# One ring of seven PSUM banks for scores, maxima and all stages, and an exponential for each head

## The chip, the core and the metric

The kernel runs on one core of one Trainium2 chip. TensorE multiplies matrices into PSUM (8 banks, each 128 partitions by 512 fp32), ScalarE computes the exponentials and other activations, VectorE reductions and element-wise work, GpSimd small steps of the layer norms and gates, SyncE issues the DMAs. The engines run their own queues in order and meet at semaphores. The metric is the device time of one execution in microseconds, as the median of several runs.

## The reference

Four layers in a row on x (4 batches, 1024 tokens, 256 features), all in fp32: a diffusion-transformer block with self-attention (16 heads of 16, a mask, rotary positions), cross-attention to 77 context tokens and an MLP; a mixture of three experts with a gate; a second such block without mask; and a last cross-attention. What matters here is the self-attention of the first and third layer:

```python
def _L2_xcond_ref(x, c, context, ...):
    x_norm = modulate(_ln(x), shift_a, scale_a)
    qkv = x_norm @ W_qkv + b_qkv
    q, k, v = jnp.split(qkv, 3, axis=-1)           # each to B, 16 heads, N, 16
    attn_w = jax.nn.softmax(jnp.einsum('bhqd,bhkd->bhqk', q, k) * scale, axis=-1)
    attn_out = jnp.einsum('bhqk,bhkd->bhqd', attn_w, v)
    x = x + gate_a[:, None] * (attn_out.transpose(0, 2, 1, 3).reshape(B, N, H) @ W_proj + b_proj)
    ...                                            # cross-attention, then the MLP
```

The mask of the first layer leaves few live keys; the program looks at it at run time and takes, with these inputs, a branch that works on the last 256 keys alone.

## The kernel before

**Stages.** The program is a preparation (to about 110 us of the trace), the first layer with few keys (region `l0_`, to about 1118), the experts (`M`, to about 1712), and the third and fourth layer (region `l2_`, to the end). In a region every engine walks the same list of tokens, `R.order`, and does its own part of each. The list is made beforehand by a planner (`overlapped`), with a cost for each token, so that the slots of self-attention alternate with the other stages: projections (`qk`, `v`, `oP`), transposes (`lnT`, `oT`), cross-attention (`cq`, `cm`, `cn`, `cs`, `cp`, `ct`) and MLP (`m1`, `m2`). The order comes from costs and dependencies only, and the list is the same before and after the change.

**A slot.** Four heads of a group are done side by side, head j on rows 32j to 32j+31 of the array. A slot with number t handles one tile of 128 keys against 512 queries. TensorE runs in it, in `slot` of `region_pe`: the scores of heads 0 and 1 (`scores(t, 0)`); for a group further on, another score product of heads 2 and 3 whose row maximum is wanted (`fill`, keys "max"); the product of the slot before with V (`pv(t - 1)`, into the accumulator, bank 7); the scores of heads 2 and 3; the maxima's products of heads 0 and 1. ScalarE makes the exponentials of the scores into `PB` (named big in the trace), VectorE reduces each "max" tile to its row maximum (`max_halves`, or `row_max` with few keys). After the last tile of a group ScalarE copies bank 7 out (`o_T`), a "tail" entry transposes it, and "nm" entries transpose the maxima.

**Banks.** Banks 0 and 1 hold the scores of two heads at a time: TensorE writes both, signals `s_full` (scores_T_full), one ACTIVATE of 128 x 1024 reads both and signals `ex` (exp_done), and only then may TensorE write the next pair (`pe.wait_ge(R.ex, R.pairs[t, half] - 1)`). Banks 2 to 6 are a ring for everything else. Each use of a bank is an entry with a running number n (`R.number`), in the order of the list; it takes bank n mod 5 of the ring, and TensorE waits in `take` until the entry 5 before has been read. Readers signal `ring_free`, TensorE `ring_full`.

**Direct slots.** Where a slot with scores is followed directly by another with no other token between them, it is in `R.single`: its heads 2 and 3 then go to two ring entries and have an exponential of 512 columns each (line 1847), and only heads 0 and 1 use banks 0 and 1 and the pair exponential (line 1842).

**Lines.** Every matmul of the helper `mm` has line 884; 1842 and 1847 are the exponentials of self-attention, 1889 those of cross-attention, 1821 the copies, 1901 the MLP's gelu; 1524 and 1522 the maxima, 1666 the cross maxima, 1589 the rows of a layer norm. ScalarE holds one table of functions at a time; going from gelu to exponential puts an ACT_TABLE_LOAD ahead of the ACTIVATE.

## Time and profile before

| | |
|---|---|
| Median of 3 runs | 3743.86 us (3739.93 to 3747.18) |
| Profiled execution | 3739.93 us, span 3738.1 us |
| TensorE busy | 3403.1 us, 91% |
| VectorE busy | 1830.6 us, 49% |
| ScalarE busy | 1394.8 us, 37% |
| Mean granted TensorE clock | 0.927 |

The profiled execution is one of the three runs. A busy share says how long at least one instruction of the engine was in flight; matmuls overlap, so TensorE's is an upper bound of its work. PE is TensorE's matmul, PEld its weight load, which can run while a matmul does. In the rows, the figure in brackets behind an instruction is the idle time of its engine just before it, and the name behind the arrow is what ended it; "issue" means that the profile shows nothing that was waited for. In fp32 each matmul of the program shows as two.

### The profile page before, as it was taken

The numbers are of one execution on the slowest core, as the hardware profiler recorded it, in microseconds if no ns is written. First come the engines' busy times: TensorE is split into PE (matmuls) and PEld (weight loads), VectorE is DVE, ScalarE is ACT, GpSimd is POOL, SyncE is SP. The second block draws the span as 40 slices with busy tenths as digits, with TensorE's granted clock in tenths as the row PEclk, the third lists the DMA queues.
The fourth block names the chain that finished last, engine by engine and source line by source line (L and its number), as shares of the span: only waits on it lengthen the run. The fifth ranks groups of instructions, "written<-read, shape, count | busy, mean of one in ns | idle before, by whom it ended". The sixth has DMA issues, their size and how long they took to land.

```text
span 3738.1 us, 49981 instructions
## 1 busy us (share of the span) xinstructions
PE 3403.1 (91%) x20564; PEld 1880.3 (50%) x20564; DVE 1830.6 (49%) x3806; ACT 1394.8 (37%) x2043; POOL 242.8 (6%) x214
## 2 busy tenths in 40 slices
PE   5798989989889999998999899999999999998887
PEld 2554665646475666665433344434354343543464
DVE  3775554452312233226766655566555665553323
ACT  0243435444312222211455444443544445445332
POOL 0100100010100000001000100000100001000010
PEclk7898989989789999998899998999999999999797
DMA  5100000002000000001000000000000000000000
GB/s 180 60 1 5 8 19 4 19 5 89 15 21 0 1 1 1 0 1 52 1 1 1 7 1 3 15 15 7 1 3 15 15 7 1 4 15 15 1 1 12
DMA packets 57258, 58.06 MB, mean 16 GB/s; under 512 B 17728, under 2 KB 51248, under 8 KB 56764
## 3 DMA queue, kind: packets, MB, share of 16 engines
q1 hardware_dynamic: 57028, 54.79, 4.8%
q8 instruction: 169, 2.77, 0.3%
q14 instruction: 61, 0.50, 0.0%
HBM read 46.89 MB, written 7.89 MB: 15 GB/s over the span
## 4 chain that ended last, share of the span: by engine, by line
PE 80%; ACT 9%; DVE 8%; issue 2%; DMA 1%; SPq 0%; POOL 0%; DVEq 0%; ACTq 0%
PE ps L884 74%; ACT big L1842 6%; PE ps L1058 2%; DVE row_max_cross L1666 2%; ACT probs L1889 2%; PE ps L1180 1%; PE ps L1038 1%; DVE max_halves L1524 1%; PE ps L1049 1%; DVE big L1672 1%; ACT L1842 1%; DVE bn_stats L1576 0%; DVE xn_tok L1589 0%; DMA big<-in_L_xcond_bss_kv 0%; DVE bn_stats L1555 0%
## 5 line engine op out<-in xcount | busy, mean ns | idle before, releaser
L884 PE MATMUL ps<-big 32*128 32x512 f32 (+2 forms) x5760 | 920.2, 622 | 59.5 <-ACT big L1842 32.4
L1842 ACT ACTIVATE big<-ps 128x1024 f32<-128x1024 f32 x548 | 562.0, 1026 | 818.9 <-PE ps L884 817.6
L1524 DVE TENSOR_REDUCE max_halves<-ps 128x1 f32<-128x512 f32 x1024 | 650.5, 684 | 423.1 <-PE ps L884 422.0
L884 PEld LDWEIGHTS ps<-big 32*128 32x128 f32 (+1 forms) x5760 | 377.4, 194 | 535.3 <-ACT big L1842 266.9
L884 PE MATMUL ps<-big,probs 128*32 128x512 f32 (+1 forms) x2688 | 387.1, 618 | 14.2 <-ACT big L1847 8.4
L884 PE MATMUL ps<-weights_mlp,big 128*128 128x256 f32 (+1 forms) x1248 | 335.6, 421 | 2.5 <-ACT big L1901 2.5
L884 PEld LDWEIGHTS ps<-weights_mlp,big 128*128 128x128 f32 x1248 | 236.0, 191 | 86.2 <-issue 59.3
L884 PE MATMUL ps<-k_v_cross,big 32*128 32x77 f32 x3072 | 144.1, 338 | 112.9 <-DVE row_max_cross L1666 63.5
L1561 DVE TENSOR_TENSOR x_tok<-ps,x_tok 128x512 f32<-128x512 f32 x112 | 77.4, 691 | 335.4 <-PE ps L884 335.3
L884 PE MATMUL ps<-x_T,weights_mlp 128*128 128x256 f32 x1024 | 233.8, 388 | 2.6 <-ACT x_T L1864 2.5
L1889 ACT ACTIVATE probs<-ps 77x512 f32<-77x512 f32 x384 | 197.1, 591 | 96.3 <-PE ps L884 96.2
L1666 DVE TENSOR_REDUCE row_max_cross<-ps 128x4 f32<-128x308 f32 x384 | 156.8, 470 | 121.7 <-PE ps L884 121.7
L884 PEld LDWEIGHTS ps<-x_T,weights_mlp 128*128 128x128 f32 x1024 | 197.2, 194 | 37.4 <-issue 5.6
L1522 DVE TENSOR_REDUCE row_max<-ps 128x2 f32<-128x512 f32 x256 | 163.0, 683 | 101.2 <-PE ps L884 100.6
L884 PE MATMUL ps<-big,k_v_cross 32*77 32x512 f32 (+1 forms) x832 | 199.8, 684 | 10.4 <-DVE big L1672 7.1
L884 PEld LDWEIGHTS ps<-k_v_cross,big 32*128 32x128 f32 x3072 | 129.8, 243 | 142.5 <-issue 101.7
L884 PEld LDWEIGHTS ps<-big,probs 128*32 128x32 f32 (+1 forms) x2688 | 76.1, 114 | 248.6 <-issue 242.3
L2037 POOL TENSOR_SCALAR eps_tile<-mean_var 128x4 f32<-128x4 f32 x56 | 13.5, 241 | 2793.3 <-DVE mean_var L1582 2793.3
L1901 ACT ACTIVATE big<-ps,mlp_b 128x256 f32<-128x256 f32 x256 | 107.5, 471 | 179.5 <-PE ps L884 179.3
L884 PE MATMUL ps<-weights,x_T 128*128 128x256 f32 x640 | 158.8, 402 | 4.7 <-ACT x_T L1821 2.5
L1847 ACT ACTIVATE big<-ps 128x512 f32<-128x512 f32 x184 | 100.0, 594 | 142.6 <-PE ps L884 142.6
L884 PEld LDWEIGHTS ps<-weights,x_T 128*128 128x128 f32 x640 | 124.9, 201 | 46.0 <-issue 22.6
(219 smaller groups left out, 3467.3 us busy)
## 6 DMA issues: line engine op xcount, KB each, us to landing
weights_mlp<-in_L_xcond_mlp_W SPq DMA_DIRECT2D x5, 1024.0 KB, 5.4
weights_mlp<-in_L_xcond_W_mlp SPq DMA_DIRECT2D x5, 1024.0 KB, 5.5
x_tok<-in_x SPq DMA_DIRECT2D x4, 1024.0 KB, 9.8
out_y<-x_tok SPq DMA_DIRECT2D x8, 512.0 KB, 2.9
big<-in_L_xcond_e_w SPq DMA_DIRECT2D x3, 1024.0 KB, 9.6
gates_biases<-mod_rows SPq DMA_DIRECT2D x20, 128.0 KB, 5.0
big<-in_L_xcond_adaLN_W SPq DMA_DIRECT2D x1, 2304.0 KB
kc_groups<-big SPq DMA_DIRECT2D x3, 616.0 KB, 4.0
```

Of the source, the lines that this page charges most:

```text
L884: return pe.matmul(out, lhsT, rhs, start=first, stop=last)
L1038: last = pe.transpose(PS[:, bank, i * P:(i + 1) * P], OT[:, c:c + P], ident[:, :])
L1049: last = pe.transpose(PS[:, bank, i * P:(i + 1) * P], NM[:, gg % 2, qt:qt + P], ident[:, :])
L1058: last = pe.transpose(PS[:, banks[ft], (t % 4) * P:(t % 4 + 1) * P], rows[:, t, ft * P:(ft + 1) * P], ident[:, :])
L1522: dve.tensor_reduce(NM[:, e, c:c + 2], PS[:, bank, :].rearrange("p (t n) -> p t n", t=2), AX.X, ALU.max, negate=True).then_inc(R.frees(key ...
L1524: dve.tensor_reduce(NMP[:, e, j, s // NH, s % NH:s % NH + 1], PS[:, bank, :], AX.X, ALU.max, negate=True).then_inc(R.frees(key), 1)
L1561: dve.tensor_tensor(x, PS[:, R.bank(key), :], x, ALU.add).then_inc(R.frees(key), 1)
L1666: dve.tensor_reduce(NMC[:, hf, g // 2, c:c + 4], src, AX.X, ALU.max, negate=True).then_inc(R.frees(key), 1)
L1842: act.activation(PB[:, score % 2, 2 * half:2 * half + 2, :], PS[:, 0:2, :], ACT.Exp, scale=SCALE).then_inc(R.ex, 1)
L1847: act.activation(PB[:, score % 2, j, :], PS[:, R.bank(key), :], ACT.Exp, scale=SCALE).then_inc(R.frees(key), 1)
L1889: act.activation(PC[0:NC, j, :], PS[0:NC, R.bank(key), :], ACT.Exp, scale=SCALE).then_inc(R.frees(key), 1)
L1901: last = act.activation(HT[hf][:, m, :], PS[:, R.bank(key), i % 2 * D:(i % 2 + 1) * D], ACT.Gelu_apprx_tanh, bias=B1[:, 0 if R.l == 0 else ...
```

## The change

Banks 0 to 6 become one ring of seven; only the accumulator keeps its own bank 7. Each head's score of every slot is a ring entry of its own, with its own `ring_full` and `ring_free`. The sets and counters of direct slots and pairs (`single`, `pairs`), and the semaphores `s_full` and `ex`, are gone. ScalarE runs one ACTIVATE of 128 x 512 for each head instead of one of 128 x 1024 for two. A slot thus has eight entries in a ring of seven, where it had four (or six, if direct) in a ring of five. The experts' stage has its own ring and is untouched.

```diff
-        RING = (2, 3, 4, 5, 6)
+        RING = (0, 1, 2, 3, 4, 5, 6)
...
                 self.order = overlapped(self) if overlap else sequential(self)
-                shown = [tok for tok in self.order if cost(self, tok)]
-                self.single = {tok[1] for tok, then in zip(shown, shown[1:]) if then[0] == tok[0] == "slot" and None not in (tok[1], then[1])}
-                self.pairs = {}
...
                     _, score, fill, pv, tails, nms = tok
-                    late = [("sc", score, 2), ("sc", score, 3)] if score in self.single else []
-                    return self.fills(fill, 0) + late + self.fills(fill, 1) + [("tail", q) for q in tails] + ...
+                    shown = [[("sc", score, j) for j in js] if score is not None else [] for js in ((0, 1), (2, 3))]
+                    return shown[0] + self.fills(fill, 0) + shown[1] + self.fills(fill, 1) + [("tail", q) for q in tails] + ...
...
                 def take(key):
                     n = R.number[key]
-                    if n >= 5:
-                        pe.wait_ge(R.ring_free[n % 5], n // 5)
-                    return RING[n % 5]
+                    if n >= 7:
+                        pe.wait_ge(R.ring_free[n % 7], n // 7)
+                    return RING[n % 7]
...
                 def scores(t, half):
-                    ring = half == 1 and t in R.single
-                    if not ring and R.pairs[t, half] > 1:
-                        pe.wait_ge(R.ex, R.pairs[t, half] - 1)
...
                     for j in (2 * half, 2 * half + 1):
-                        rows, bank = slice(32 * j, 32 * j + 32), take(("sc", t, j)) if ring else j % 2
+                        rows, bank = slice(32 * j, 32 * j + 32), take(("sc", t, j))
...
-                    if not ring:
-                        last.then_inc(R.s_full, 1)
...
                 def pv(t):
-                    if t in R.single:
-                        pe.wait_ge(R.ex, R.pairs[t, 0])
-                        for j in (2, 3):
-                            pe.wait_ge(*R.freed(("sc", t, j)))
-                    else:
-                        pe.wait_ge(R.ex, R.pairs[t, 1])
+                    for j in range(HG):
+                        pe.wait_ge(*R.freed(("sc", t, j)))
...
                     if score is not None:
-                        for half in range(1 if score in R.single else 2):
-                            act.wait_ge(R.s_full, R.pairs[score, half])
-                            if half == 0 and score >= 2:
-                                act.wait_ge(R.pv, score - 1)
-                            act.activation(PB[:, score % 2, 2 * half:2 * half + 2, :], PS[:, 0:2, :], ACT.Exp, scale=SCALE).then_inc(R.ex, 1)
...
+                        if score >= 2:
+                            act.wait_ge(R.pv, score - 1)
+                        for j in range(HG):
+                            key = ("sc", score, j)
+                            act.wait_ge(*R.full(key))
+                            act.activation(PB[:, score % 2, j, :], PS[:, R.bank(key), :], ACT.Exp, scale=SCALE).then_inc(R.frees(key), 1)
```

No engine's instructions change places; what each waits for does. The order below is the built program's, row by row, with the semaphores each row waits for. First TensorE in region `l2_`, at a slot behind the first half of an MLP (the place at 2216 us of the trace): two scores and two maxima, the product with V, two scores and two maxima, and then a product of cross-attention. Before:

```order
L884 MATMUL ps<-big 128x512 [waits l2_ring_free1,l2_exp_done]
L884 MATMUL ps<-big 128x512
L884 MATMUL ps<-big 128x512 [waits l2_ring_free4]
L884 MATMUL ps<-big 128x512 [waits l2_ring_free0]
L884 MATMUL ps<-big,probs 32x512 [waits l2_exp_done]
L884 MATMUL ps<-big,probs 32x512 x3
L884 MATMUL ps<-big 128x512 [waits l2_exp_done]
L884 MATMUL ps<-big 128x512
L884 MATMUL ps<-big 128x512 [waits l2_ring_free1]
L884 MATMUL ps<-big 128x512 [waits l2_ring_free2]
```

And after, at the same place:

```order
L878 MATMUL ps<-big 128x512 [waits l2_ring_free4,l2_ring_free3]
L878 MATMUL ps<-big 128x512 [waits l2_ring_free5]
L878 MATMUL ps<-big 128x512 [waits l2_ring_free6]
L878 MATMUL ps<-big 128x512 [waits l2_ring_free0]
L878 MATMUL ps<-big,probs 32x512 [waits l2_ring_free3,l2_ring_free4,l2_ring_free0,l2_ring_free6]
L878 MATMUL ps<-big,probs 32x512 x3
L878 MATMUL ps<-big 128x512 [waits l2_ring_free1]
L878 MATMUL ps<-big 128x512 [waits l2_ring_free2]
L878 MATMUL ps<-big 128x512 [waits l2_ring_free3]
L878 MATMUL ps<-big 128x512 [waits l2_ring_free4]
```

The third bundle (last four rows) waited for the slot's own pair exponential, exp_done. Now each row waits for a bank of its own; only the last, ring_free4, is the bank of this slot's first row. The product waits for four heads instead of one pair.

Second, ScalarE at the same place: the gelu of the MLP, the table load, the exponentials of the slot, and the copy of the accumulator. Before:

```order
L1901 ACTIVATE big<-ps,mlp_b 128x256 [waits l2_ring_full2] x2
L1901 ACTIVATE big<-ps,mlp_b 128x256 [waits l2_ring_full3] x2
L1842 ACT_TABLE_LOAD [waits l2_pv_done]
L1842 ACTIVATE big<-ps 128x1024 [waits l2_scores_T_full] x2
L1821 ACTIVATE o_T<-ps 128x512 [waits l2_ring_full3,l2_pv_done]
```

After:

```order
L1881 ACTIVATE big<-ps,mlp_b 128x256 [waits l2_ring_full2] x2
L1881 ACTIVATE big<-ps,mlp_b 128x256 [waits l2_ring_full3] x2
L1827 ACT_TABLE_LOAD [waits l2_ring_full4]
L1827 ACTIVATE big<-ps 128x512 [waits l2_pv_done]
L1827 ACTIVATE big<-ps 128x512 [waits l2_ring_full5]
L1827 ACTIVATE big<-ps 128x512 [waits l2_ring_full1]
L1827 ACTIVATE big<-ps 128x512 [waits l2_ring_full2]
L1805 ACTIVATE o_T<-ps 128x512 [waits l2_ring_full2,l2_pv_done]
```

Two exponentials have become four, and the table load, which stood behind the wait for an older product (pv_done) and ahead of that for the scores, now stands behind the wait for the score of head 0 (ring_full4).

Third, TensorE where slots follow each other directly (the stretch from 1797 to 2097 us of the trace): the third bundle of one slot and the first of the next. Before:

```order
L884 MATMUL ps<-big 128x512 [waits l2_ring_free1]
L884 MATMUL ps<-big 128x512 [waits l2_ring_free2]
L884 MATMUL ps<-big 128x512 [waits l2_ring_free3]
L884 MATMUL ps<-big 128x512 [waits l2_ring_free4]
L884 MATMUL ps<-big 128x512 [waits l2_exp_done]
L884 MATMUL ps<-big 128x512
L884 MATMUL ps<-big 128x512 [waits l2_ring_free0]
L884 MATMUL ps<-big 128x512 [waits l2_ring_free1]
```

After:

```order
L878 MATMUL ps<-big 128x512 [waits l2_ring_free4]
L878 MATMUL ps<-big 128x512 [waits l2_ring_free5]
L878 MATMUL ps<-big 128x512 [waits l2_ring_free6]
L878 MATMUL ps<-big 128x512 [waits l2_ring_free0]
L878 MATMUL ps<-big 128x512 [waits l2_ring_free1]
L878 MATMUL ps<-big 128x512 [waits l2_ring_free2]
L878 MATMUL ps<-big 128x512 [waits l2_ring_free3]
L878 MATMUL ps<-big 128x512 [waits l2_ring_free4]
```

In both, the last row (the maximum of head 3 of the next slot) waits for the bank of the first row (the score of head 2 of this slot). The two rows that waited for exp_done now wait for two banks of the ring.

## Rows read from the trace of the kernel before

**Rows 1.** The page: busy time, share of the span and instructions; then the chain's shares by engine, by line.
```profile
PE 3403.1 (91%) x20564; PEld 1880.3 (50%) x20564; DVE 1830.6 (49%) x3806; ACT 1394.8 (37%) x2043; POOL 242.8 (6%) x214
...
PE 80%; ACT 9%; DVE 8%; issue 2%; DMA 1%; SPq 0%; POOL 0%; DVEq 0%; ACTq 0%
PE ps L884 74%; ACT big L1842 6%; PE ps L1058 2%; DVE row_max_cross L1666 2%; ACT probs L1889 2%; PE ps L1180 1%; PE ps L1038 1%; DVE max_halves L1524 1%; PE ps L1049 1%; DVE big L1672 1%; ACT L1842 1%; DVE bn_stats L1576 0%; DVE xn_tok L1589 0%; DMA big<-in_L_xcond_bss_kv 0%; DVE bn_stats L1555 0%
```

**Rows 2.** Timeline, alternating stretch: start, length, engine, line, operation, count, [idle before, what ended it].
```profile
2216.28 1.14 PE L884 MATMUL ps<-big 32*128 32x512 f32 x8
...
2217.24 1.28 ACT L1842 ACT_TABLE_LOAD   x1
...
2218.54 1.02 ACT L1842 ACTIVATE big<-ps 128x1024 f32<-128x1024 f32 x1
2219.61 0.31 PEld L884 LDWEIGHTS ps<-big 32*128 32x128 f32 x8 [2.11 <-ACT big L1842]
...
2222.93 0.16 PEld L884 LDWEIGHTS ps<-big,probs 128*32 128x32 f32 x8 [0.76 <-issue]
...
2223.04 1.02 ACT L1842 ACTIVATE big<-ps 128x1024 f32<-128x1024 f32 x1 [0.25 <-PE ps L884]
...
2224.11 0.31 PEld L884 LDWEIGHTS ps<-big 32*128 32x128 f32 x8 [1.02 <-ACT big L1842]
```

**Rows 3.** Waits, whole trace: who waited for whom, us in total, times, longest.
```profile
PEld ps L884 <- ACT big L1842: 269.0, 250, 2.1
...
PE ps L884 <- DVE row_max_cross L1666: 63.5, 44, 3.4
...
PEld ps L884 <- DVE max_halves L1524: 45.5, 77, 3.7
```

**Rows 4.** Waits from 1797 to 2097 us, then from 2097 to 3487 us.
```profile
PEld ps L884 <- ACT big L1842: 10.8, 12, 1.0
...
PEld ps L884 <- ACT big L1842: 205.3, 193, 2.1
```

**Rows 5.** Timeline, directly followed slots, 1882.6 to 1886.6 us.
```profile
1882.67 0.31 PEld L884 LDWEIGHTS ps<-big 32*128 32x128 f32 x8 [0.84 <-issue]
...
1883.63 0.20 PEld L884 LDWEIGHTS ps<-big 32*128 32x128 f32 x3 [0.23 <-issue]
1883.83 1.09 ACT L1847 ACTIVATE big<-ps 128x512 f32<-128x512 f32 x2 [1.85 <-PE ps L884]
...
1884.48 0.29 PEld L884 LDWEIGHTS ps<-big 32*128 32x128 f32 x2 [0.64 <-ACT big L1847]
1884.80 1.03 ACT L1842 ACTIVATE big<-ps 128x1024 f32<-128x1024 f32 x1
1885.53 0.16 PEld L884 LDWEIGHTS ps<-big,probs 128*32 128x32 f32 x8 [0.76 <-issue]
...
1886.52 0.20 PEld L884 LDWEIGHTS ps<-big 32*128 32x128 f32 x4 [0.84 <-issue]
```

**Rows 6.** The page's costliest groups: count, busy us, mean ns, idle before.
```profile
L1842 ACT ACTIVATE big<-ps 128x1024 f32<-128x1024 f32 x548 | 562.0, 1026 | 818.9 <-PE ps L884 817.6
...
L1847 ACT ACTIVATE big<-ps 128x512 f32<-128x512 f32 x184 | 100.0, 594 | 142.6 <-PE ps L884 142.6
```

**Rows 7.** Line 1842 alone: least, median and greatest length, first and last start.
```profile
L1842 ACT ACT_TABLE_LOAD  x22: 1283/1283/1283, 402.9 to 3296.5; - x22
```

**Rows 8.** Timeline, first layer, ScalarE's table load ahead of a slot.
```profile
703.68 1.28 ACT L1842 ACT_TABLE_LOAD   x1
...
714.25 1.03 ACT L1842 ACTIVATE big<-ps 128x1024 f32<-128x1024 f32 x1 [9.29 <-PE ps L884]
```

**Rows 9.** Windows: span, busy us (instructions) by engine, granted clock, DMA share, GB/s.
```profile
110.00:1118.00 1008.00, 909.07 (x6019) 599.53 (x6018) 507.81 (x1098) 380.26 (x578) 83.10 (x76) 0.91 0.07 21
...
1797.30:2097.70 300.40, 294.52 (x1860) 103.56 (x1853) 201.81 (x350) 150.46 (x213) 6.15 (x7) 1.00 0.00 1
2097.70:3487.00 1389.30, 1279.33 (x8820) 591.87 (x8816) 761.90 (x1485) 643.63 (x859) 102.51 (x73) 0.95 0.03 8
```

More of the change, by code:

```diff
@@ L295, in __init__ @@
                         self.adds[add] = len(self.adds)
-                self.ring_full, self.ring_free = (sems(name + side, "0 1 2 3 4") for side in ("ring_full", "ring_free"))
-                self.s_full, self.ex, self.pv, self.acc, self.nm, self.rec, self.crec = sems(name, "scores_T_full exp_done pv_done acc_out max_done recip cross_recip")
+                self.ring_full, self.ring_free = (sems(name + side, "0 1 2 3 4 5 6") for side in ("ring_full", "ring_free"))
+                self.pv, self.acc, self.nm, self.rec, self.crec = sems(name, "pv_done acc_out max_done recip cross_recip")
                 self.ln_st, self.ln_mv, self.ln_ep, self.ln_rs, self.ln_norm = sems(name + "ln_", "stats mean_var eps rstd rows")
@@ L330, in entries @@
                     _, score, fill, pv, tails, nms = tok
[L331 to L332 removed]
+                    shown = [[("sc", score, j) for j in js] if score is not None else [] for js in ((0, 1), (2, 3))]
+                    return shown[0] + self.fills(fill, 0) + shown[1] + self.fills(fill, 1) + [("tail", q) for q in tails] + [("nm", g, hf) for g in nms for hf in range(NH)]
                 if kind in ("lnT", "oT"):
@@ L1837, in slot @@
                     if score is not None:
-                        for half in range(1 if score in R.single else 2):
-                            act.wait_ge(R.s_full, R.pairs[score, half])
-                            if half == 0 and score >= 2:
-                                act.wait_ge(R.pv, score - 1)
-                            act.activation(PB[:, score % 2, 2 * half:2 * half + 2, :], PS[:, 0:2, :], ACT.Exp, scale=SCALE).then_inc(R.ex, 1)
-                        if score in R.single:
-                            for j in (2, 3):
-                                key = ("sc", score, j)
-                                act.wait_ge(*R.full(key))
-                                act.activation(PB[:, score % 2, j, :], PS[:, R.bank(key), :], ACT.Exp, scale=SCALE).then_inc(R.frees(key), 1)
+                        if score >= 2:
[4 more added lines that the diff above has]
+                            act.activation(PB[:, score % 2, j, :], PS[:, R.bank(key), :], ACT.Exp, scale=SCALE).then_inc(R.frees(key), 1)
                     if product is not None and (product + 1) % R.per == 0:
```

19 lines of the change are left out of this document (7 added, 12 removed).

## The prediction

> **What bounds the kernel now.** I read the page first. TensorE is busy 91% of the span and holds 80% of the chain that ended last; ScalarE is busy 37% and VectorE 49% [rows 1]. So the time is TensorE's work plus what TensorE waits for. The second name on the chain is the exponential of the big layers, line 1842, with 6% [rows 1]: TensorE waits for it often, though ScalarE has time to spare. That is the wait this change touches, so everything hangs on how long it is net of what TensorE would have been doing anyway.
>
> The timeline of one such place shows it [rows 2]. A slot is three bundles on TensorE: the scores of heads 0 and 1 with the maxima of heads 2 and 3 (four row groups side by side), the product with V, and the scores of heads 2 and 3 with the maxima of heads 0 and 1. The product's weights are loaded at 2222.93, those of the third bundle at 2224.11, 1.18 later. That load came after 1.02 of idle and was released by the exponential of line 1842, which ran 2223.04 to 2224.06. Between two slots that follow each other directly the same weight load comes after 0.84 idle with nothing to wait for ("issue"), 0.99 after the product's [rows 5]. So the wait on the path is 1.02 - 0.84 = 0.18 us, not the whole exponential: the product with V covers the rest.
>
> **The sum over all such places.** The list of waits has weight loads released by line 1842 for 269.0 us in 250 places [rows 3]. Taking off 0.84 for each, which passes there anyhow, leaves 269.0 - 210.0 = 59.0 us. By stretch: 205.3 us in 193 places from 2097 to 3487, the part in which slots alternate with other stages [rows 4], is 43.2 us net; 10.8 us in 12 places from 1797 to 2097, where slots follow each other directly [rows 4], is 0.7 us net; the remaining 52.9 us in 45 places lie in the first layer and are 15.1 us net. No more than these 59 us can come back directly.
>
> **The change, part by part.**
>
> *Scores of slots followed by other work.* These are 228 of 320 slots: line 1847 ran 184 times, two for each of 92 directly followed slots, and line 1842 548 times, of which 548 - 92 = 456 are two for each other slot [rows 6]. Their third bundle waited for the slot's own first exponential (exp_done in the first pair of fences on the order). Now each head takes the next of seven banks, and the entry seven back was freed long before: in the new order it is the last head of the slot before, or a maximum. In the third bundle only the last maximum (head 0 and 1 come last) still points at this slot: it takes the bank of head 0's score. That one is read by an exponential of 512 columns, 0.594 against 1.026 mean [rows 6], so it is free 0.43 earlier than the pair was. A wait of 0.18, or of anything up to 0.43, goes entirely; a longer one shrinks by 0.43.
>
> ScalarE loads the exponential's table 22 times at this line [rows 7]; 20 of these loads are followed at once by an exponential whose scores are already there. At 2217.24 the load takes 1.28, the exponential ends at 2219.56, and the third bundle's weight load is idle 2.11, thus 1.27 net [rows 2]. Some 20 of these are at most 20 x 1.27 = 25 us of the 59. The other 230 waits are the remaining 34 us, 0.15 each.
>
> *The table load moves behind the wait.* On ScalarE the order of the waits changes: before, the load stood behind the wait for an old product and ahead of the wait for the scores; now the wait for head 0's score stands ahead of the load (second pair of fences). At 2217.24 the load starts 0.18 before the bundle's scores are full (TensorE's bundle, 2216.28 + 1.14 = 2217.42) [rows 2]. So of the 0.43 regained there 0.18 is lost: 20 x 0.25 = 5 us. In the two other places the load ran long before its exponential, as at 703.68, 10.6 us ahead of it [rows 8]; there its 1.28 now falls on the path, less 0.43: 2 x 0.85 = 1.7 us lost.
>
> *Where the first bundle waited.* After a single short stage between two slots the first bundle waited for the slot's second exponential. Its last maximum now takes the bank of head 3's score, read by the last of four exponentials. That is the same moment plus about 0.06 (two of 512 take 1.09 together, one of 1024 takes 1.03 [rows 5]), so these places gain nothing. I put them at 4 us of the 34: fifteen places or so near 0.2 to 0.3.
>
> *Slots that follow each other.* The period there is 3.86 us (1882.67 to 1886.52), and the last two weight loads of the first bundle are released by line 1847 after 0.64 idle [rows 5]: the fourth tile starts at 1884.48 where its three neighbours started their first pass at 1883.63, 0.85 earlier. This looks like the prize of two more banks, but it is not to be had. Before, with six entries to a slot in five banks, the maximum of head 3 took the bank of head 2's score of the slot before; now, with eight entries to a slot in seven banks, it takes the very same one (third pair of fences: the wait in the last row is for the bank of the first). 92 places, no change; had it gone, it would be up to 92 x 0.85 = 78 us.
>
> *ScalarE's own work.* 456 + 92 = 548 pair instructions become 1096 of 512. Two back to back take 1.09 against 1.03, so 548 x 0.06 = 33 us more on an engine idle 63% of the span [rows 1, 5]. Alone it costs nothing on the path; it is in the 0.06 above. The Trainium skill ("ScalarE: Activation LUTs", section "What ACT_TABLE_LOAD costs") says that an activation with immediate scale costs a fixed 186 ns plus 0.833 ns per column, of which 93 ns overlap back to back: a split pair would be 0.093 longer rather than 0.06. The trace's 1.09 is nearer 0.06; either way it lies beside TensorE's work.
>
> *More waits in TensorE's queue.* A product of such a slot waits on four semaphores instead of one. Products behind three waits started as soon after the bundle as the others do (0.76 idle, "issue", in rows 5, and 0.76 in rows 2): zero, at most 3 x 0.05 x 228 = 34 us if an extra wait cost 0.05, an estimate from above that the equal 0.76 excludes.
>
> *Sum.* Short waits 34 - 4 = 30, table loads 5 - 1.7 = 3, together 33 us taken off. Not all reaches the end. TensorE also waits on chains that run through VectorE (PE released by the cross maxima 63.5 us, by max_halves 45.5 [rows 3]); where it arrives 0.2 earlier at such a wait, the 0.2 is given back. These are some 120 places against 228 slots; I take off a sixth, 5 us. 3739.9 (the profiled execution's own time; its span is 3738.1) - 28 = 3712. The profiled run was the fastest of three, 3.9 below the median of 3743.9, so 3712 to 3716 are one answer; I say 3713.
>
> **The rivals.**
>
> *A. The waits move and little is left (20%).* TensorE stops waiting for the exponential and arrives earlier at the next wait. For it: the chain runs through several engines, and the net waits are only 0.18. Against it: TensorE is busy 1279 of 1389 us in the alternating stretch [rows 9], so most bundles follow their predecessor at once. If three quarters are given back, 3740 - 8 = 3732 to 3742.
>
> *B. VectorE becomes the scores' gate (8%), slower.* A score now needs a bank that VectorE may hold: maxima, cross maxima, and in front of them in its queue the rows of a layer norm. Before, scores waited for ScalarE alone and could pass a late VectorE. Place: the alternating stretch, where VectorE is 55% busy (761.9 of 1389.3) [rows 9]. It decides once the new waits average over 33/228 = 0.15 us per slot; at 0.3 per slot the time would be 3740 - 33 + 68 = 3775. Against it: TensorE's bundles wait for max_halves in 77 places only, 45.5 us [rows 3], and a bank is asked for again only after seven more entries, nearly a whole slot of some 3 us.
>
> *C. The clock (6%).* The granted clock is 1.00 (2.4 GHz throughout) in the stretch of direct slots, and as a mean with 1.2 GHz passages 0.95 in the alternating one and 0.91 in the first layer [rows 9]. If finer hand-overs took the alternating stretch from 0.95 to 0.91, 4% of its 1279 us, 51 us, come on top: 3763. The other way, to 0.97, 26 us go: 3687; I give that 6% more. The Trainium skill ("TensorE: Matmul & The Clock Gate", section "A second HAM failure mode: psum-queue depth-cycling") says that cycling through PSUM banks in each iteration leaves small idles in which the clock oscillates. By that rule the direct stretch, a ring of five already, should oscillate; the trace disagrees, with 1.00 over 300 us.
>
> *D. It doesn't do what it says.* Excluded for the scores: the order shows the waits replaced. It holds for the direct slots, and is in the sum.
>
> **How the numbers follow.** Forecast, 3695 to 3731, 60%; A 20%; B 8%; C slower 6%, C faster 6%. Range 3686 to 3741: below, all 59 less the 4 and 1.7 regained, 3687; above, A's end. Less than 2 in 10 are outside. What a measurement of this kernel can tell from no change is about 0.2%, 7.5 us. Faster than 3736.4: forecast, C faster and a third of A, 0.72. Within: most of A, 0.16. Slower: B, C, 0.12.
>
> **What would show it.** Right: in the changed profile the third bundle starts 0.99 after the product in the alternating stretch, with its weight load idle 0.84 by "issue"; waits released by the exponential fall from 269 us to the 92 direct places and the table loads; the period of direct slots stays 3.86; ScalarE's busy time grows by 30 to 90 us; table loads start after the scores' bundle. Wrong: the direct period falls below 3.8 (then the time is near 3650), weight loads of scores released by VectorE (B), or the clock of 2097 to 3487 off 0.95 by more than 0.02 (C).

## The result and the profile after

| | before | after |
|---|---|---|
| Median | 3745.12 us (3739.93 to 3747.18, 4 runs) | 3588.17 us (3576.93 to 3596.79, 4 runs) |
| Ratio, 95% interval | 1 | 0.9576 [0.9557, 0.9595] |
| Profiled execution, its span | 3739.93, 3738.1 us | 3596.79, 3594.9 us |
| Mean granted TensorE clock of it | 0.927 | 0.937 |

The change takes 157 us off the median, where the prediction had 28 to 31. The profiled execution of after is the slowest of its four, so the two traces differ by 143 us only, and what follows accounts for these 143. One run of the kernel before, beside the last three experiments, took 4909 us at a granted clock of 0.63; it is left out of every ratio and moves the median it stands in from 3742.1 to 3743.9.

The page after; it answers to [rows 1] and [rows 6]:

```profile
PE 3371.6 (94%) x20564; PEld 1877.9 (52%) x20564; DVE 1829.8 (51%) x3806; ACT 1422.3 (40%) x2591; POOL 242.5 (7%) x214
...
PE 90%; DVE 6%; ACT 2%; issue 1%; DMA 1%; SPq 0%; POOL 0%; DVEq 0%; ACTq 0%
PE ps L878 83%; PE ps L1042 3%; PE ps L1164 1%; PE ps L1022 1%; PE ps L1033 1%; ACT probs L1869 1%; DVE row_max_cross L1650 1%; ACT big L1827 1%; DVE bn_stats L1560 1%; DVE max_halves L1508 1%; PE ps L1142 0%; DMA big<-in_L_xcond_bss_kv 0%; DVE xn_tok L1573 0%; DVE row_max L1506 0%; DVE big L1656 0%
...
L1827 ACT ACTIVATE big<-ps 128x512 f32<-128x512 f32 x1280 | 687.3, 598 | 824.9 <-PE ps L878 824.2
```

TensorE now holds 90% of the chain instead of 80%, and the exponential (now line 1827) 1% instead of 6%. ScalarE is busy 27.5 us longer for its 548 more instructions, on an engine that has the time. TensorE's idle time (span less busy) went from 335.0 to 223.3, thus by 111.7. Its busy time went from 3403.1 to 3371.6 with the same 20564 matmuls: that is 31.5 us of the same work done faster, at a higher clock or with fewer stalls inside a bundle, where one of four tiles comes late and the others still count as busy.

The waits of TensorE after, against [rows 3]:

```profile
PEld ps L878 <- DVE max_halves L1508: 93.9, 131, 4.1
...
PEld ps L878 <- ACT big L1827: 67.3, 122, 0.9
...
PE ps L878 <- DVE row_max_cross L1650: 31.5, 44, 2.9
```

Line 1827 now holds the exponentials of both old lines, and line 1847 had a wait of its own before:

```profile
PEld ps L884 <- ACT big L1847: 34.9, 62, 0.6
```

So the weight loads released by an exponential of self-attention fell from 303.9 us (269.0 + 34.9) to 67.3. The waits for VectorE's maxima of the cross-attention halved, 63.5 to 31.5, in 44 places before and after, though neither these maxima nor their products were edited; only the number of banks was. The third wait grew, 45.5 to 93.9, a rise of 48.4 us. Of that rise 43.2 lie in the direct slots below (2.0 to 45.2), where it names 0.76 us that were called "issue" before and passed anyway.

Where the time went, stage by stage. The ends of the stages were read from the same instructions in both traces; the rows are windows (span, busy us of PE, PEld, DVE, ACT, POOL with instructions, granted clock, DMA share, GB/s). First layer with slots, first layer's tail without slots, direct slots of the third layer, third and fourth layer with slots, last tail without slots. Before:

```profile
173.90:901.00 727.10, 673.58 (x4720) 425.22 (x4720) 392.04 (x825) 311.20 (x458) 52.29 (x48) 0.93 0.03 9
901.00:1092.40 191.40, 166.09 (x964) 120.59 (x964) 54.95 (x132) 53.98 (x104) 14.94 (x12) 0.89 0.15 49
...
1803.50:2077.60 274.10, 272.07 (x1717) 94.84 (x1716) 182.50 (x309) 139.26 (x201) 3.62 (x3) 1.00 0.00 1
2077.60:3483.30 1405.70, 1293.86 (x8888) 596.62 (x8888) 772.84 (x1512) 651.05 (x867) 105.04 (x77) 0.95 0.03 8
3483.30:3738.10 254.80, 208.25 (x1308) 134.17 (x1308) 85.84 (x205) 70.28 (x131) 18.10 (x15) 0.79 0.02 5
```

After:

```profile
175.30:865.20 689.90, 667.33 (x4720) 428.13 (x4720) 392.56 (x825) 315.65 (x566) 52.24 (x48) 0.95 0.03 9
865.20:1045.80 180.60, 160.44 (x964) 116.38 (x964) 55.12 (x132) 53.82 (x104) 14.91 (x12) 0.91 0.16 52
...
1755.50:2028.20 272.70, 271.67 (x1720) 95.79 (x1724) 182.32 (x309) 143.41 (x272) 3.62 (x3) 1.00 0.00 1
2028.20:3360.00 1331.80, 1289.09 (x8888) 604.46 (x8888) 772.02 (x1512) 670.23 (x1230) 104.98 (x77) 0.96 0.03 9
3360.00:3594.90 234.90, 195.13 (x1308) 126.24 (x1308) 85.44 (x205) 69.76 (x131) 18.12 (x15) 0.82 0.02 5
```

The differences are 37.2, 10.8, 1.4, 73.9 and 19.9 us; the rest of the program is 0.0 together (the stretch before the first slots 1.4 longer, the experts 1.8 longer, the start of the third layer 3.2 shorter). Two tails in which no slot runs, and no exponential of line 1842, gave 30.7 us. That alone is about as much as the whole forecast.

In the third and fourth layer with slots TensorE's idle time (the stretch less its busy time) went from 111.8 to 42.7 us. The list of waits, for the matmuls in these two windows alone, says what had ended it. Before:

```profile
PE ps L884 <- DVE row_max_cross L1666: 29.4, 21, 2.7
PE ps L884 <- ACT big L1842: 23.6, 40, 1.2
PE ps L884 <- DVE max_halves L1524: 19.9, 16, 3.6
```

After:

```profile
PE ps L878 <- ACT big L1827: 17.2, 19, 1.2
PE ps L878 <- DVE row_max_cross L1650: 13.8, 20, 1.9
PE ps L878 <- DVE max_halves L1508: 5.8, 2, 3.3
```

With 8.4 us of line 1847 added to the rows before, the exponentials' part fell by 14.8 us (32.0 to 17.2), and that of VectorE's two kinds of maxima by 29.7 (49.3 to 19.6). Even among the slots, more idle time went at readers that the change had not touched than at the exponentials. (Idle time leaves out a stall inside a bundle, of which an example follows.)

The direct slots after, against [rows 5] (timeline):

```profile
1838.25 0.31 PEld L878 LDWEIGHTS ps<-big 32*128 32x128 f32 x8 [0.84 <-issue]
...
1839.41 2.06 ACT L1827 ACTIVATE big<-ps 128x512 f32<-128x512 f32 x4 [1.79 <-PE ps L878]
...
1840.06 0.29 PEld L878 LDWEIGHTS ps<-big 32*128 32x128 f32 x2 [0.64 <-ACT big L1827]
1841.11 0.16 PEld L878 LDWEIGHTS ps<-big,probs 128*32 128x32 f32 x8 [0.76 <-DVE max_halves L1508]
...
1842.10 0.31 PEld L878 LDWEIGHTS ps<-big 32*128 32x128 f32 x8 [0.84 <-issue]
```

The period is 3.85 (1838.25 to 1842.10) and the fourth tile still waits 0.64 for the exponential: here the new ring maps to the same bank, as forecast.

An alternating place after, with a table load, against [rows 2] (timeline):

```profile
2180.84 1.28 ACT L1827 ACT_TABLE_LOAD   x1 [0.26 <-PE ps L878]
...
2181.70 2.20 PE L878 MATMUL ps<-big 32*128 32x512 f32 x8
2182.13 2.07 ACT L1827 ACTIVATE big<-ps 128x512 f32<-128x512 f32 x4
2182.78 0.29 PEld L878 LDWEIGHTS ps<-big 32*128 32x128 f32 x2 [0.77 <-ACT big L1827]
...
2186.48 0.16 PEld L878 LDWEIGHTS ps<-big,probs 128*32 128x32 f32 x8 [0.76 <-issue]
...
2187.48 0.31 PEld L878 LDWEIGHTS ps<-big 32*128 32x128 f32 x8 [0.84 <-issue]
```

At 2187.48 the third bundle starts 1.00 after the product with nothing to wait for. At 2180.84 the load begins only once a score is there, 0.26 after the gelu before it. The third bundle of that slot starts at 2181.70, but its last tile waits until head 0's exponential has ended (0.77 idle at 2182.78). So the bundle takes 2.20 where one without such a wait takes 1.14. These 1.06 us stand where 1.27 net of idle time stood before; they now count as busy.

The cross maxima, in which four entries are filled side by side and VectorE reduces the four. Before (timeline):

```profile
2097.78 1.64 DVE L1666 TENSOR_REDUCE row_max_cross<-ps 128x4 f32<-128x308 f32 x4 [0.67 <-PE ps L884]
...
2099.18 2.00 PE L884 MATMUL ps<-k_v_cross,big 32*128 32x77 f32 x32 [1.38 <-DVE row_max_cross L1666]
...
2102.57 2.01 PE L884 MATMUL ps<-k_v_cross,big 32*128 32x77 f32 x32 [1.39 <-DVE row_max_cross L1666]
```

After, same place:

```profile
2048.19 1.64 DVE L1650 TENSOR_REDUCE row_max_cross<-ps 128x4 f32<-128x308 f32 x4 [0.84 <-PE ps L878]
...
2048.82 2.00 PE L878 MATMUL ps<-k_v_cross,big 32*128 32x77 f32 x32 [0.57 <-DVE row_max_cross L1650]
...
2051.44 2.00 PE L878 MATMUL ps<-k_v_cross,big 32*128 32x77 f32 x32 [0.61 <-DVE row_max_cross L1650]
```

With five banks the next group of four has one free bank and needs three of the four reductions; its products start 1.40 after VectorE does. With seven it has three free banks and needs one reduction; it starts 0.63 after. The same wait is 0.8 us shorter, and from group to group it is 2.62 us (2048.82 to 2051.44) instead of 3.39 (2099.18 to 2102.57).

### The profile page after: what moved, and what is told of

It reads as the page before. It is cut to its first block, busy times and chain, and to the rows that moved or that the text cites. A ratio compares the mean times of both kernels' runs of the same rounds, so it can differ in the third digit from the quotient of the medians.

```text
span 3594.9 us, 51053 instructions
## 1 busy us (share of the span) xinstructions
PE 3371.6 (94%) x20564; PEld 1877.9 (52%) x20564; DVE 1829.8 (51%) x3806; ACT 1422.3 (40%) x2591; POOL 242.5 (7%) x214
## 4 chain that ended last, share of the span: by engine, by line
PE 90%; DVE 6%; ACT 2%; issue 1%; DMA 1%; SPq 0%; POOL 0%; DVEq 0%; ACTq 0%
PE ps L878 83%; PE ps L1042 3%; PE ps L1164 1%; PE ps L1022 1%; PE ps L1033 1%; ACT probs L1869 1%; DVE row_max_cross L1650 1%; ACT big L1827 1%; DVE bn_stats L1560 1%; DVE max_halves L1508 1%; PE ps L1142 0%; DMA big<-in_L_xcond_bss_kv 0%; DVE xn_tok L1573 0%; DVE row_max L1506 0%; DVE big L1656 0%
## 5 line engine op out<-in xcount | busy, mean ns | idle before, releaser
L1827 ACT ACTIVATE big<-ps 128x512 f32<-128x512 f32 x1280 | 687.3, 598 | 824.9 <-PE ps L878 824.2
L878 PE MATMUL ps<-big 32*128 32x512 f32 (+2 forms) x5760 | 950.5, 614 | 13.8 <-DVE row_max L1506 5.2
L878 PEld LDWEIGHTS ps<-big 32*128 32x128 f32 (+1 forms) x5760 | 392.9, 192 | 491.3 <-issue 385.7
L878 PE MATMUL ps<-k_v_cross,big 32*128 32x77 f32 x3072 | 130.1, 314 | 56.9 <-DVE row_max_cross L1650 31.5
L878 PE MATMUL ps<-big,k_v_cross 32*77 32x512 f32 (+1 forms) x832 | 167.1, 684 | 6.9 <-DVE big L1656 6.9
L878 PEld LDWEIGHTS ps<-k_v_cross,big 32*128 32x128 f32 x3072 | 116.4, 220 | 85.0 <-issue 71.4
L878 PE MATMUL ps<-weights,big 128*128 128x256 f32 x640 | 145.5, 380 | 0.0
```

The lines of the kernel that those rows point to most:

```text
L878: return pe.matmul(out, lhsT, rhs, start=first, stop=last)
L1827: act.activation(PB[:, score % 2, j, :], PS[:, R.bank(key), :], ACT.Exp, scale=SCALE).then_inc(R.frees(key), 1)
```

## The experiments

Four causes were put against each other: the split of the exponential alone; the ring of seven (R in the expectations), in the end narrowed to the wider ring of the other stages (W); the place of the table load (T); and the order in which banks are taken. Ratios stand against runs of the kernel before on the same chip (medians 3743.90 to 3745.34). Differences from after are differences of medians, and mostly of runs on different chips.

### The split alone: before, with an exponential and a semaphore for each head

```diff
-                    if not ring and R.pairs[t, half] > 1:
-                        pe.wait_ge(R.ex, R.pairs[t, half] - 1)
                     for j in (2 * half, 2 * half + 1):
...
+                        if not ring and R.pairs[t, half] > 1:
+                            pe.wait_ge((R.ex, R.ex1)[j % 2], R.pairs[t, half] - 1)
```

The scores stay in banks 0 and 1, the ring has five.

> One part of the change alone: the kernel before, with banks 0 and 1 kept for the scores and the ring of five for the rest, but an exponential of 512 columns for each head and a semaphore for each of the two banks. Theory R (the two more banks are what pays, for scores and for the other stages alike): the second score of a half still waits for the second of two exponentials, which ends 0.06 us later than the pair of 1024 did, so nothing is gained: 3735 to 3755 us. Rival S (the size of the exponential is what pays): the first score starts 0.43 us earlier in 228 slots, and most of the 157 us comes: 3600 to 3690 us.

Measured: 3755.29 us (3749.91 to 3770.83), ratio 1.0036 [1.0017, 1.0055], just at the upper end of theory R. The split alone gains nothing; it costs 10. The layers with slots: 1414.6 us against 1405.7 before. So an exponential that is finished 0.43 sooner helps only together with the ring.

### The ring of seven in the tails alone

```diff
+                    bank = 2 + n % 5 if n < self.slots_end else (n - self.slots_end) % 7
```

Before, unchanged up to the last slot of each region; behind it the idle banks 0 and 1 join the ring.

> The kernel before, unchanged as long as there are slots, but after the last slot of each of the two regions the ring has banks 0 to 6 instead of 2 to 6. No exponential of a score is left there. After the last slot the changed kernel is 20 us (third and fourth layer) and 11 us (first layer) shorter. Theory R: cross attention and MLP by themselves are held by five banks: 31 us go, 3705 to 3725 us. Rival S (all of the gain is the scores' wait, and what the rest shows is the clock, which comes out another way): 3737 to 3750 us.

Measured: 3706.10 us (3704.37 to 3709.16), ratio 0.9904 [0.9887, 0.9920]. 39 us from stages that have no slot at all, within theory R. The two tails and the layers with slots:

```profile
902.30:1080.60 178.30, 156.34 (x964) 115.40 (x964) 55.36 (x132) 53.81 (x104) 14.90 (x12) 0.93 0.16 53
2064.50:3470.40 1405.90, 1294.13 (x8888) 596.49 (x8888) 773.07 (x1512) 650.42 (x867) 104.94 (x77) 0.95 0.03 8
3470.40:3704.90 234.50, 196.71 (x1308) 127.21 (x1308) 85.88 (x205) 69.76 (x131) 18.09 (x15) 0.81 0.02 5
```

The layers with slots take their 1405.9 as before, the tails 13 and 20 us less (33 of the 39; the two traces differ by no more). This part of the gain is separate and fully reproduced without touching an exponential.

### After with six banks

```diff
-        RING = (0, 1, 2, 3, 4, 5, 6)
+        RING = (1, 2, 3, 4, 5, 6)
```

(and 7 becomes 6 in the modulus).

> The changed kernel with six banks in its ring instead of seven (bank 0 is left unused). In direct slots the last maximum of the first bundle then takes the bank of head 3's score, read 0.49 us later: 92 x 0.49 = 45 us more; in the others the last maximum of the third bundle waits for the second exponential of its own slot, as before the change, some 25 us more. These 70 us come by either theory: 3658 us. Theory R adds the other stages' waits for banks, some 20 to 40 us: 3675 to 3700 us. Rival S adds nothing: 3650 to 3665 us.

Measured: 3757.70 us (3751.82 to 3761.64), ratio 1.0035 [1.0021, 1.0050]: 170 more than after, where theory R had 87 to 112 and rival S less. The seventh bank carries more than the whole gain. The direct slots and the layers with slots:

```profile
1801.30:2098.10 296.80, 296.62 (x1719) 109.92 (x1719) 186.89 (x308) 143.47 (x272) 3.62 (x3) 1.00 0.00 1
2098.10:3513.90 1415.80, 1359.12 (x8888) 654.78 (x8888) 774.08 (x1512) 672.51 (x1230) 104.92 (x77) 0.95 0.03 8
```

The direct slots lose 24 us at a clock of 1.00 and show no more idle time (0.2 us): eight entries in six banks make two tiles of a bundle wait (0.64 and then 0.20 us, at 1833.42 and 1833.91) where in seven it is one, and a bundle with one tile at work counts as busy. So busy time is no measure here of what TensorE could do; PE is busy 70 us longer in the layers with slots for the same 8888 matmuls.

### After with the hand-over by pairs

```diff
                     if n >= 7:
+                        prior = R.listed[n - 7]
+                        if prior[0] == "sc" and prior[2] % 2 == 0:
+                            pe.wait_ge(*R.freed(prior[:2] + (prior[2] + 1,)))
...
+                            act.wait_ge(*R.full(("sc", score, j | 1)))
```

The ring stays seven; ScalarE starts a pair only when both scores are there, and TensorE takes a bank of the pair only when both are read.

> The changed kernel with its ring of seven, but exponentials that act as pairs: head 0's (or 2's) begins only when its neighbour's score is there too, and its bank counts as free only when the neighbour's is. This undoes the finer hand-over alone. Theory R: the third bundle's last maximum waits again for the pair, 0.18 us in some 130 slots and more at 20 table loads, in direct slots the first bundle waits 0.49 longer in 92 places (45 us); the waits of the other stages stay short: 3588 + 65 = 3640 to 3665 us. Rival S: the size is what pays, all is back near the time before: above 3700 us.

Measured: 3714.62 us (3711.12 to 3716.53), ratio 0.9925 [0.9909, 0.9942], 126 more than after, where R expected 52 to 77. The time falls into the range of rival S (above 3700 us), so the hand-over by head carries much more than R gave it. Only 30 us of the gain are left. A direct slot of this kernel (timeline):

```profile
1855.78 0.16 PEld L879 LDWEIGHTS ps<-big,probs 128*32 128x32 f32 x8 [0.76 <-issue]
...
1859.20 0.29 PEld L879 LDWEIGHTS ps<-big 32*128 32x128 f32 x2 [1.25 <-ACT big L1832]
1860.25 0.16 PEld L879 LDWEIGHTS ps<-big,probs 128*32 128x32 f32 x8 [0.76 <-issue]
```

The last tile waits 1.25 instead of 0.64, and the period is 4.47 (1855.78 to 1860.25) instead of 3.85. Of the 126 us 31 lie in the direct slots, which the change itself did not move; there the experiment adds a wait that before never had. The layers with slots lose 67 and go back to 1399.2, nearly the 1405.7 of before. So the ring does not do without the hand-over by head, nor the split, in the first experiment, without the ring.

### Other stages held to five banks

```diff
+                    open_banks = range(7) if key[0] in ("sc", "max", "tail", "nm") else range(2, 7)
+                    bank = min(open_banks, key=lambda i: (stamp[i], i))
```

After; scores and maxima of the slots use all seven banks, every other stage only 2 to 6; each entry takes the permitted bank that was given out longest ago. With all seven permitted that is the ring of after.

> The changed kernel, with seven banks for scores, maxima and the two kinds of transposes inside a slot, while the other stages (projections, layer-norm transposes, cross attention, MLP) may use banks 2 to 6 only, the least recently used first. Undoes the wider ring for the other stages alone. Theory W (the wider ring for them is a part of its own beside the scores' hand-over): after the last slots the 31 us come back, and among the slots the waits for cross maxima, cross probabilities and maxima too (before to after, TensorE's idle time ended by these fell by some 60 us in all): 3640 to 3670 us. Rival V (among the slots only the scores' hand-over counts): the 31 us alone, 3612 to 3625 us.

Measured: 3724.03 us (3706.84 to 3743.97, 8 runs), ratio 0.9955 [0.9933, 0.9977]: 136 more than after, where W had 52 to 82; the runs spread over 37 us. The wait for the cross maxima is back to that of before:

```profile
PE ps L889 <- DVE row_max_cross L1661: 64.3, 44, 3.2
```

The restriction also shifts which banks the scores take: weight loads released by their exponentials wait 85.5 us instead of 67.3. So not all of the 136 lie in the other stages.

### Cross-attention alone held to five banks

```diff
+                    bank = min(range(2, 7) if key[0] in ("cm", "cs") else range(7), key=lambda i: (stamp[i], i))
```

> The changed kernel with one kind of stage held to five banks: the cross maxima and cross scores, which take four banks at a time each, may use banks 2 to 6 only. Everything else has seven. Theory W (the wider ring pays where cross attention takes four banks and then four again, and the next group of four waits for VectorE's or ScalarE's reading): most of what the restriction of all other stages cost, 136 us, comes with these alone: 3670 to 3724 us. Rival: the restriction costs in every stage alike, and cross attention has a third of it: 3620 to 3640 us.

Measured: 3686.14 us (3675.75 to 3690.01), ratio 0.9840 [0.9817, 0.9863], 98 more than after, within theory W. Two kinds of entries, the cross maxima's (cm) and the cross scores' (cs), carry 98 of the 136:

```profile
PE ps L888 <- DVE row_max_cross L1660: 63.8, 44, 3.1
...
PE ps L888 <- ACT probs L1879: 22.6, 20, 1.7
```

Both waits have their old size (before 63.5 and, for the cross probabilities, 22.8), together 40 us more than in after, while the scores' own waits hardly move (69.4 against 67.3). The two traces differ by 89.4 us (3684.3 - 3594.9): TensorE's idle time is 50.0 longer, most of it these 40, and its busy time 39.4 longer for the same matmuls. The mean clock of this profile is 0.926 against 0.937, thus (1 - 0.926) x 3684 = 273 us against (1 - 0.937) x 3595 = 226: up to 47 us of slower clock could hold the busy time. That is a bound and not a measurement.

### The table load ahead of the scores' wait

```diff
-                        if score >= 2:
-                            act.wait_ge(R.pv, score - 1)
                         for j in range(HG):
                             key = ("sc", score, j)
                             act.wait_ge(*R.full(key))
+                            if j == 0 and score >= 2:
+                                act.wait_ge(R.pv, score - 1)
```

In this program, of the two waits written ahead of the first exponential the one written last lands ahead of the load, and the other stays with the ACTIVATE (the pair of fences on ScalarE's order). So in after the load stands behind the wait for the score; here it stands, as in the kernel before, behind that for the old product and ahead of the score's. ScalarE's idle time ahead of the 22 loads shows it (last number, us), in after and in this kernel:

```profile
L1827 ACT ACT_TABLE_LOAD x22 | 28.2, 1283 | 20.3 <-PE ps L878 20.3
...
L1827 ACT ACT_TABLE_LOAD x22 | 28.2, 1283 | 0.4
```

Of the 20.3 us 14.3 lie at the two loads whose exponential has to wait for its scores anyway (3.71 and 10.62); at the other twenty it is 0.26 to 0.47.

> The changed kernel with the waits ahead of a slot's first exponential in the order of the kernel before, so that a table load stands ahead of the wait for the score. Theory T (as predicted): 20 loads start 0.18 us earlier and two fall off the path with 1.28: 5 to 7 us less, 3581 to 3584 us. Rival: TensorE runs ahead of these loads by the wider ring and nothing changes, 3586 to 3591 us.

Measured: 3568.33 us (3560.80 to 3570.06), ratio 0.9527 [0.9514, 0.9539], 20 less than after, where T had 4 to 7. At the place that answers to 2181.70 in after, the third bundle is held 0.24 us less:

```profile
2168.27 1.96 PE L878 MATMUL ps<-big 32*128 32x512 f32 x8
```

Twenty times 0.24 is 5 us, and 1.28 at each of the two other loads makes 7: T's own sum. The other 13 us are not in these places. The layers with slots:

```profile
2016.50:3329.30 1312.80, 1269.69 (x8888) 595.21 (x8888) 771.94 (x1512) 670.03 (x1230) 105.03 (x77) 0.97 0.03 9
```

TensorE's idle time there is 43.1 (1312.8 - 1269.7) as in after, 42.7; the 19 us are all in busy time, at a granted clock of 0.97 instead of 0.96. But this trace is the fastest of its five runs and that of after the slowest of its four, and the runs of after differ by 20 us among themselves (3576.93 to 3596.79, at 0.942 to 0.936). So the two traces can't say how much of the 19 comes from the edit.

### The same, the other way round, in the kernel before

```diff
-                            act.wait_ge(R.s_full, R.pairs[score, half])
                             if half == 0 and score >= 2:
                                 act.wait_ge(R.pv, score - 1)
+                            act.wait_ge(R.s_full, R.pairs[score, half])
```

> The kernel before with one edit: ahead of a slot's first exponential the waits stand in the order of the changed kernel, so that the table load stands behind the wait for the scores. In the changed kernel the reverse edit gave 20 us, of which 20 x 0.18 and 2 x 1.28 make 6 us directly. Theory T: 6 us and no more are the table loads' own, the rest was the granted clock, which falls behind small idle times; before, where TensorE idles more anyhow, the cost is 5 to 12 us: 3750 to 3757 us. Rival (the later table load costs 20 us by itself): 3762 to 3770 us.

Measured: 3764.01 us (3756.47 to 3773.17), ratio 1.0055 [1.0033, 1.0076]: 20 us slower than before, from the late load alone, as the rival had it; the interval allows 12 to 28. The idle time ahead of the loads, before and here:

```profile
L1842 ACT ACT_TABLE_LOAD x22 | 28.2, 1283 | 0.4
...
L1842 ACT ACT_TABLE_LOAD x22 | 28.2, 1283 | 20.6 <-PE ps L884 20.6
```

In this pair much of the loss is idle time. The traces differ by 24.5 us, of which TensorE's idle time is 15.9 (335.0 to 350.9); the weight loads released by line 1842 wait 284.2 us instead of 269.0. So by medians the order of two waits is worth some 20 us in either kernel. The change as made has this loss in it, and gained its 157 in spite of it.

### Banks by expected time instead of in turn

```diff
+                            bank = min(range(7), key=lambda i: (max(ready[i], clock - 3.0), i))
```

Each entry takes the bank that a small model of the readers' queues expects to be read first: once on after, once with the early table load.

> The changed kernel with another choice of bank for each entry: not the next in turn but the one that should be read first, by a list of fixed reading times per kind (score 0.5, maximum 0.63, cross maximum 0.48 and so on, from the traces). Seven banks and the order of the work stay. Theory W: a fixed turn makes entries wait for late readers while another bank is free already, above all the last maximum of a first bundle behind a single stage, which waits for head 3's exponential though head 0's maximum is reduced 0.4 us before it: 35 such places, 14 us, and a little in other stages: 3565 to 3580 us. Rival: in most places all seven banks are in use and the turn is the order of reading anyhow: 3583 to 3595 us. In direct slots the period stays 3.86 in both, as the first read of the bundle before is still the first bank to come free.

Measured: 3614.99 us (3610.03 to 3626.20), ratio 0.9660 [0.9644, 0.9676], 27 more than after and outside both ranges.

> The two edits before together, the order of the waits and the choice of banks. If both theories hold they add: 20 us less than the changed kernel, 3568 us. If neither does, 3588 us.

Measured: 3617.49 us (3615.19 to 3627.69), ratio 0.9664 [0.9649, 0.9678], 49 more than with the load alone. The plain ring is better than this choice, with or without the load. The model, not the idea, may be at fault; that stays open.

### The accumulator's bank in the tails, the best version

```diff
+                    bank = min(range(8 if n >= self.slots_end else 7), key=lambda i: (stamp[i], i))
```

On top of the early table load, bank 7 joins the ring behind the last slot.

> The changed kernel with the table load ahead of the wait for the score (measured at 3568 us), and after the last slot of each region the accumulator's bank joins the ring as the eighth. Two more banks there gave 31 to 39 us. Theory W: one more gives some more, 5 to 12 us: 3556 to 3563 us. Rival (seven are enough for two groups of four, and what waits remain come from the chain of cross attention): no change, 3565 to 3572 us.

Measured: 3552.59 us (3551.17 to 3554.14), ratio 0.9488 [0.9469, 0.9507], 16 us less than with the load alone, 36 less than after. W had 5 to 12; the two profiled runs, each the fastest of its five, differ by 9.6. The last tail took 229.6 us with seven banks and now takes

```profile
3330.40:3549.40 219.00, 180.98 (x1308) 118.94 (x1308) 84.60 (x205) 69.73 (x131) 18.14 (x15) 0.88 0.02 6
```

## Why the prediction was wrong

**The step that failed** is the sentence "No more than these 59 us can come back directly." It summed only the waits that the exponential of line 1842 released. But the change has two halves, and the second, two more banks for every other stage, has no term in the sum. The row for it was there: 63.5 us in 44 places for the cross maxima [rows 3]. The prediction used it only as a place where time would be *given back*. It fell to 31.5, and in five banks for cross-attention alone the loss was 98 us, in five for all other stages 136, in six for everything 170. In the tails, where the forecast was nothing, came 31 us (39 when done alone). In the third and fourth layer with slots VectorE's maxima gave TensorE 29.7 us of idle time back, the exponentials 14.8. The three signs of being wrong could not show this: each looks at the scores, the direct slots or the clock, and none at the other stages.

**The short waits.** The mechanism was right where a slot has no table load: the third bundle now starts 1.00 after the product, without a wait. The waits by the exponentials went from 303.9 to 67.3 us, not to "the 92 direct places and the table loads" by the prediction's count. The stretch of direct slots has 53 such places and 30.6 us (before 61 places and 38.0), the rest lies at the table loads and elsewhere. But the layers with slots gained 73.9 and 37.2 us where the net waits were 43 and 15. The split alone brings none of it (3755.29), and with the hand-over by pairs most of it is lost (3714.62). The gain of the two halves is no sum: 30 us are left without the hand-over by head, 21 without the banks of the others, 157 come with both. (Of what the hand-over by pairs loses, 31 us lie in direct slots, where the change had gained nothing; without these 61 would be left.) Why they need each other is argued and not shown: in a shared ring a bank held longer delays whichever entry comes seven later, so every reader must be short and the ring deep.

**Direct slots.** Right: period 3.85, 272.7 us against 274.1. The ring of six and the hand-over by pairs show how near the edge it lies: 24 and 31 us more.

**The table load.** The direction was right, and so was the size at one place: the sum left 0.25 us of gain (0.43 less 0.18), and the trace shows 0.21 (1.27 net before, 1.06 after). Priced as a loss, the late load was 20 x 0.18 and 2 x 1.28, some 6 us; both experiments measured 20. What the other 13 or so are stays open.

**ScalarE, queued waits, VectorE.** Nearly right: 27.5 us more busy time (33 forecast, 30 as the lower end of the sign) lie beside TensorE's work; products behind four waits still start after 0.76. Rival B, VectorE as the scores' gate, did not show: of the 48.4 us by which its releases grew, 43.2 are the direct slots' 0.76 that passed anyway.

**The clock.** It was treated as a rival with a chance of its own, at 51 or 26 us, and not as part of each term. It rose from 0.927 to 0.937, and (1 - clock) x span went from 273 to 226 us. This 47 overlaps with the idle time and cannot be added to it. Rival C's other way, "to 0.97, 26 us go", had the direction right for the stretch, which went from 0.95 to 0.96, and left out the tails (0.79 to 0.82, 0.89 to 0.91). It was not what made the difference: busy time in that stretch fell by 4.8 us, idle time by 69.1.

**The give-back** of a sixth can't be told apart in the total: the stages gained more than their net waits, and the waits for VectorE's maxima, at which time was to be given back, shrank.

## What to carry to other kernels

When a change gives buffers to everyone, go through every wait on a buffer, by whoever releases it, and not only those of the step that gave it up; here the waits in untouched code were worth as much as those aimed at (136 us lost with five banks for the other stages, 126 with the hand-over by pairs). Count how many buffers the widest group takes at once (four) and ask whether the ring holds the next group beside it (three free of seven, one free of five). Where a lookup table is loaded, put the wait that is over first ahead of it and the late one behind it; that was worth some 20 us here, though not all of it was traced.

## What the runs showed that was not expected

- The order of two waits on ScalarE, ahead of 22 table loads, is worth some 20 us by medians in both kernels (3568.33 against 3588.17; 3764.01 against 3743.90), where the places themselves explain about 7. In the kernel before, 15.9 of the 24.5 us between the traces are idle time of TensorE. Between after and the early load the traces show no such idle time, but they come from the slow and the fast end of the runs.
- The mean granted clock goes with the time only loosely, with the same matmuls: the kernels here at 3740 us and more have 0.922 to 0.927, the two fastest 0.946, but the five banks for other stages have 0.925 at 3707, cross-attention in five 0.926 at 3686, and the hand-over by pairs 0.936 at 3713. The runs do not say which stalls bring the clock down to its lower level of 1.2 GHz, only that the stretch of direct slots, which stalls a tile in most periods of 3.85 us or more, had a mean granted clock of 1.00 in every kernel whose window was read, the ring of six (296.8 us) and the pairs (303.8 us) among them.
- A bundle of four tiles side by side hides the stall of one of them from the busy time: in the ring of six TensorE's idle time in the layers with slots was 56.7 us (1415.8 - 1359.1) against 111.8 before (1405.7 - 1293.9), and yet they took 10 us longer.
